# Splitting the per-pair selective-scan step of a Mamba layer into two halves, one pair apart

## What is computed

```python
def mamba(x):                       # W_in 1024x4096, DI = 2048
    xc, z = split(x @ W_in)
    u = silu(causal_depthwise_conv4(xc))
    dt_raw, B_raw = split(u @ W_x)  # 16 + 16
    dt = clip(softplus(dt_raw @ W_dt + b_dt), 1e-4, 1.0)
    ub = u * (B_raw @ W_Bp)
    h[t] = h[t-1] * (1 - dt[t]) + ub[t]
    y = (h + D_param * u) * silu(z)
    return y @ W_out
x = x + mamba(ln(x))
x = x + ffn(ln(x))                  # silu(x wg') * (x wu') @ wd', hidden 3072
x = x + attn(ln(x))                 # causal, one head of 1024, own residual
x = x + ffn(ln(x))
```

## Time and profile before

| | us |
|---|---|
| median of 2 runs | 3411.22 (3409.91 to 3412.52) |
| profiled execution | 3419.05 |
| its span on the slowest core (core 0) | 3417.5 |
| spans of the 8 cores | 3383.0 to 3417.5 |
| PE busy, of that span | 2018.6 (59%) |
| DVE busy | 956.0 (28%) |
| ACT busy | 776.5 (23%) |
| POOL busy | 323.6 (9%) |

### The profile page before, as it was taken

One profiled execution on the slowest core, in us unless ns is written; L12 is line 12 of the kernel. 1 busy time (PEld: TensorE's weight loads), 2 busy tenths in 40 slices (PEclk: granted clock), 3 DMA queues, 4 the chain that ended last, 5 costly groups with the idle time before them and its releaser, 6 DMA issues.

```text
span 3417.5 us, 29901 instructions; the slowest of 8 cores (3383.0 to 3417.5 us)
## 1 busy us (share of the span) xinstructions
PE 2018.6 (59%) x9275; PEld 984.6 (29%) x9432; DVE 956.0 (28%) x1617; ACT 776.5 (23%) x1196; POOL 323.6 (9%) x404
## 2 busy tenths in 40 slices
PE   1355555455554520764859577129677486859687
PEld 0233333333333210321324233014333142324232
DVE  3234444444444430102212120444322121211121
ACT  0244544445444423201101010100000110101010
POOL 0211222122222210021000000000000000000000
PEclk9576666676676655886989989559877698989889
DMA  7200000000000039243030302540211503030303
GB/s 243 73 13 25 1 25 7 19 25 1 25 7 19 22 123 289 77 136 120 16 108 1 98 26 71 172 154 1 86 51 48 181 23 101 13 111 1 110 13 96
DMA packets 69851, 233.31 MB, mean 68 GB/s; under 512 B 8450, under 2 KB 8578, under 8 KB 67652
## 3 DMA queue, kind: packets, MB, share of 16 engines
q10 hardware_dynamic: 35712, 112.21, 9.9%
q1 hardware_dynamic: 27460, 91.92, 8.9%
q0 software_dynamic: 6528, 27.27, 2.0%
HBM read 170.55 MB, written 60.82 MB: 68 GB/s over the span
## 4 chain that ended last, share of the span: by engine, by line
PE 38%; DMA 21%; DVE 13%; ACT 9%; issue 8%; DVEq 4%; POOLq 3%; POOL 2%; ACTq 2%; SPq 0%
PE ps_s L976 15%; DMA arena<-wd_c 6%; PE ps_s L942 5%; DVEq L143 4%; DMA arena<-xs 4%; PE ps_s L1046 3%; PE ps L1314 3%; PE ps L1046 3%; POOLq L143 2%; ACT L679 2%; POOL arena L560 2%; DVE arena L516 2%; PE ps_s L1261 2%; PE ps L759 2%; PE ps_s L1224 2%
## 5 line engine op out<-in xcount | busy, mean ns | idle before, releaser
L976 PE MATMUL ps_s<-arena 128*128 128x512 bf16 x2256 | 506.3, 385 | 10.8 <-DVE arena L328 8.6
L584 PE MATMUL ps_s<-arena 128*128 128x256 bf16 x1024 | 213.3, 396 | 336.8 <-ACT arena L508 334.4
L318 PE MATMUL ps<-arena 128*128 128x128 bf16 x512 | 63.5, 307 | 488.9 <-DVE arena L307 488.9
L976 PEld LDWEIGHTS ps_s<-arena 128*128 128x128 bf16 x2304 | 227.9, 99 | 287.8 <-issue 24.7
L1046 PE MATMUL ps_s<-arena 128*128 128x512 bf16 x752 | 210.4, 400 | 142.7 <-DMA arena<-wd_c 93.7
L266 ACT ACTIVATE arena<-arena 128x1024 bf16<-128x1024 f32 x64 | 67.6, 1057 | 917.2 <-DMA arena<-xs 826.4
L584 PEld LDWEIGHTS ps_s<-arena 128*128 128x128 bf16 x1024 | 136.5, 137 | 406.3 <-issue 353.7
L942 PE MATMUL ps_s<-arena 128*128 128x512 bf16 x752 | 170.3, 387 | 119.7 <-ACT arena L952 62.9
L499 PE MATMUL ps_s<-arena 128*128 128x256 bf16 x1024 | 172.9, 342 | 112.6 <-DVE arena L447 62.4
L991 DVE TENSOR_TENSOR arena<-arena,ps_s 128x512 bf16<-128x512 f32 x144 | 99.0, 688 | 422.2 <-ACT arena L985 422.2
L1046 PE MATMUL ps<-arena 128*128 128x512 bf16 x752 | 210.8, 402 | 0.9
(11 more groups left out here) (93 smaller groups left out, 2393.0 us busy)
## 6 DMA issues: line engine op xcount, KB each, us to landing
xs<-arena ACTq DMA_DIRECT2D x48, 512.0 KB, 2.9
arena<-xs ACTq DMA_DIRECT2D x48, 512.0 KB, 4.4
arena<-wd_c SPq DMA_DIRECT2D x84, 256.0 KB, 2.6
arena<-wd_c ACTq DMA_DIRECT2D x84, 256.0 KB, 2.6
arena<-wg_t SPq DMA_DIRECT2D x16, 768.0 KB, 6.2
arena<-wu_t SPq DMA_DIRECT2D x16, 768.0 KB, 6.6
arena<-x ACTq DMA_DIRECT2D x16, 512.0 KB, 4.6
arena<-w_in ACTq DMA_DIRECT2D x8, 1024.0 KB, 10.7
```

The source lines that it names most:

```text
L318: lambda e, s=xn_bf_tile, dj=dj, pbf=pbf: e.transpose(pbf[:, dj * P:(dj + 1) * P], s[:, dj * P:(dj + 1) * P], g_ident),
L584: lambda e, dj=dj, ci=ci, bkx=bkx, half=half, par=par: e.matmul(psb[bkx][:, half * TCM:(half + 1) * TCM], win_bf[:, dj * 4096 + ci * P: dj ...
L976: lambda e, hi=hi, dj=dj, bk=bk, par=par, wsrc=wsrc: e.matmul(psb[bk], wsrc[:, dj * H + hi * P: dj * H + (hi + 1) * P], fxnt[par][:, dj * ...
```

## The change

`phaseB_pair` becomes two functions. `phaseB1(k, pi)` holds the small matmuls, L674, the ACT chain and L691; `phaseB2(k, pi)` holds L697, the scan, L722, POOL's work and now, at its end, `wout_t0(k, pi)` of the same pair. The loop has nine steps: step `pi` emits B1 of pair `pi`, then B2 and phase A of pair `pi-1`. An unused view, `wd_pair`, goes. The computation and the waits are the same otherwise.

```diff
-        def phaseB_pair(k, pi):
+        def phaseB1(k, pi):
             ...
             mk_mm = s_pe.mark()
-            if pi >= 1:
-                wout_t0(k, pi - 1)
             em.op("vector",
             ...
-            mk_sp2 = mk_sp2_hist[(k, pi)] = s_se.mark()
+            mk_sp2_hist[(k, pi)] = s_se.mark()
             ...
             mk_ubm_hist[(k, pi)] = s_ve.mark()
+
+        def phaseB2(k, pi):
+            ci0 = 2 * pi
+            pp = pi % 2
+            prev_gp = mk_gp_hist.get((k, pi - 2)) or \
+                (mk_gp_hist.get((k - 1, 6 + pi)) if k > 0 else None)
             em.op("vector", lambda e, pp=pp: e.tensor_scalar(
                 a_f[pp][:], a_f[pp][:], 0.9999, None,
-                op0=ALU.min), wait=[mk_sp2], drain=False)
+                op0=ALU.min), wait=[mk_sp2_hist[(k, pi)]], drain=False)
             ...
             mk_gp_hist[(k, pi)] = s_gp.mark()
+            wout_t0(k, pi)
             ...
         for k in range(NKM):
-            for pi in range(8):
-                phaseB_pair(k, pi)
-                if k + 1 < NKM:
-                    phaseA_xc_pair(k + 1, pi)
-                    phaseA_z_pair(k + 1, pi)
+            for pi in range(9):
+                if pi < 8:
+                    phaseB1(k, pi)
+                if pi >= 1:
+                    phaseB2(k, pi - 1)
+                    if k + 1 < NKM:
+                        phaseA_xc_pair(k + 1, pi - 1)
+                        phaseA_z_pair(k + 1, pi - 1)
             if k + 1 == NKM - 1:
                 mk_xz_last = s_pe.mark()
-            wout_t0(k, 7)
             mamba_tail(k)
```

More of the change, by code:

```diff
@@ L815, in ffn @@
             wd_sb = [VA(F_WD + i * 2048, 2048, BF16) for i in range(2)]
-            wd_pair = VA(F_WD, 4096, BF16)
             fxA = [VA(F_XIN2 + i * 4096, 4096, F32) for i in range(NTF)]
```

## The result

The changed kernel takes 3451.84 us (median of 11 runs) for 3411.22 us of the kernel before; the ratio is 1.0117, with a 95% interval of 1.0084 to 1.0149: slower by a little over 1%, less than 2%. Some executions of every kernel here are several per cent slower at a lower granted clock, so the medians in this document are over all executions and the ratios over the others alone. The forecast was 3465 us in a range of 3412 to 3512. The two profiled executions took 3419.05 and 3443.83 us, 24.8 us apart; runs of one kernel differ by 13 us and more themselves (3399.29 to 3436.03 before, 3443.83 to 3456.39 after), so where the time went is read from stretches of the trace, and these repeat closely.

What follows compares the result with a forecast made beforehand. A ring through TensorE, closed by L643 waiting for y of the same pair, was to bound each step at 14.7 us; seven chunks (+40 us) and chunk 7 (+14) gave +54, 3465 us on the median, range 3412 to 3512.

Steps and rivals of the forecast that it cites:

- Ring one: Pair loop of ScalarE copy, DVE, GpSimd, SiLU and decay chain: 14.62 us before, some 11 us once split.
- the second ring: Loop through TensorE: L643 waits for same-pair y, behind DVE and the small matmuls; 16.4 us at the low clock.
- the signs that the prediction named: L643 waits for L735 in almost every pair, TensorE idle 5 to 6 us; first L508 15 us after L659.
- The step: One pair's round in chunks 0 to 6: 14.4 us with the clock rising, mean 14.7 us.
- one step in six: Share of pair steps expected to stay at the low clock throughout, raising the mean from 14.4 to 14.7 us.
- 5.78 + 0.5: Per step: 5.78 us of DVE and GpSimd work with TensorE idle, plus 0.5 us hold of L697 by L560.
- Fill, last step, end: Per chunk: 9.8 us before the first L643, 12.7 to the last burst, 8.6 from there to release.
- Chunk 7: Last chunk, with no next chunk to project: 66.6 us for 52.46, so +14 us.
- The tail: L747 to L769, the store and next layer norm after each chunk: unchanged, the edit costs nothing there.
- The low ring: Rival: clock stays low or the hold shifts each burst; steps 16.4 us, 3550 us in all; chance 0.18.
- The short ring: Rival: clock rises early, no hold on L697; steps 13.8 us, 3421 us in all; chance 0.16.
- The faster case: Rival: clock stays high across 5.8 us of idle; steps 12.4 us, chunks 101.3, 3332 us; chance 0.06.

Runs made afterwards that it cites:

- experiment 1: Changed kernel with the split kept, but output matmuls L643 again those of the pair before: 3218.10 us, ratio 0.9406.
- experiment 2: Changed kernel with the split kept, L643 of the same pair moved from ahead of L499 to behind L584: 3246.82 us, ratio 0.9484.
- experiment 3: Kernel before, not split, with L643 of the same pair placed ahead of L499: 3771.25 us in the profiled execution, no ratio.
- experiment 5: Changed kernel plus 26 matmuls into an unused bank ahead of each L643 in chunks 0 to 6: 3359.85 us, ratio 0.9850.

## Why the prediction was right

**The bound.** Ring one opened as forecast (57.6 to 0.4 us of wait), and the second ring closed in its place (52.8 us of L643 on y). Experiments 1 and 2 show that L643's place closes it, experiment 3 that it is the costly half. The "some 11 us" of the opened ring one came out as 11.1 to 11.4 in experiment 1. Of the signs that the prediction named, the wait of L643 was there in all eight pairs of chunk 1, and the first L508 of a chunk came 14.5 to 15.2 us after its L659; only the idle time ahead of L643 was above the 5 to 6 us given.

**The step.** 14.7 us forecast; measured 14.5 us in chunk 1 (87.3 us for six steps, from 342.9 to 430.2), which is the longest chunk, and 14.4 in the mean of all seven. Within it two terms were off and in part cancelled, which was luck. I had one step in six stay low altogether, worth 0.3 us; in none did it. In chunk 1 the clock rose in L499 or in the pause behind it every time (2.55 to 3.62 us for L499), and all of L584 took 1.91, as in the other six chunks. Against that the idle part was 6.4 to 6.7 us in these six steps, mean 6.5, and not 5.78 + 0.5: the hold on the clip was 0.55 to 0.83, and 0.05 us was missing in the releases.

In chunk 1 the hold is each time some 0.15 us less than what is left of the GpSimd instruction: at 367.14 us L560 had 0.70 us to go, and the clip lost 0.55. The prediction read the two L516 of the earlier trace rows as losing just what was left of L735; they lost 0.92 us, and 1.12 were left (357.44 + 1.15 less 357.47). The durations of the clip show the hold (minimum, median, maximum in ns; it was 426 to 428 in all 64 of before):

```profile
L701 DVE TENSOR_SCALAR arena<-arena x64: 417/980/1261, 195.4 to 1240.6; 128x512 f32<-128x512 f32 x64
```

**Fill, last step, end.** 9.8, 12.7 and 8.6 us forecast; 9.9, 12.8 and 7.5 measured in chunk 1, and 9.8, 13.1 and 7.7 in the mean of seven. The end was shorter since L584 was at the high clock there too. Per chunk 119.3 us forecast, 116.7 measured: +3.2 for +5.7.

**Chunk 7.** 66.6 us forecast, 67.6 measured: +15.2 for +14.

**The tail** is the one step whose reasoning failed: "so this edit costs nothing" stood for L747 to L769, and the tail got shorter. Seven such stretches took 8.6 to 10.3 us before, 65.2 in sum, and 8.6 to 9.0 after, 60.6 in sum. Before, the output matmuls of the second half (L759) began at the low clock in three of the seven chunks and took 8.50 to 8.75 us there, for 7.07 in the other four. Chunk 0 of before:

```profile
304.96 1.02 PE L643 MATMUL ps<-arena 128*128 128x512 bf16 x4 [0.71 <-POOL arena L735]
...
307.52 8.56 PE L759 MATMUL ps<-arena 128*128 128x512 bf16 x31 [1.54 <-DVE arena L747]
```

The same chunk after, where L764 is L759 and takes 6.85 us in all seven chunks:

```profile
304.71 1.91 PE L584 MATMUL ps_s<-arena 128*128 128x256 bf16 x16 [0.82 <-ACT arena L508]
...
308.38 6.85 PE L764 MATMUL ps<-arena 128*128 128x512 bf16 x31 [1.76 <-DVE arena L752]
```

So before, L643 still ran at the high clock (1.02 us for four), and it was gone after 1.54 us of idle time; in the other four chunks the same pause did not bring it down, nor did the 1.76 us after the change. Why is not shown. These 4.6 us and 2.4 us from elsewhere between the chunks, which I did not trace, are the 7 us that came back. With the shorter chunks they make the difference between +54 forecast and +30.5 in the Mamba layer. The direction and the mechanism were right; of the 54 us forecast 40.6 are there between the medians and 24.8 between the profiled executions.

**The rivals.** The low ring (16.4 us a step) did not come, as no step stayed low. The short ring (13.8) did not either, as the hold was there in all six steps of every chunk. The faster case needed a clock that outlasts the idle time; it did not, but experiment 5, which fills that time, came to its numbers: 12.45 us a step for 12.4, chunks of 102.8 for 101.3.

**A hold in the last step.** No row of before showed an instruction with two SBUF inputs held by GpSimd. The changed kernel has one in the last step of a chunk, where the scans of pair 7 meet the two GpSimd sums of pair 6 (here chunk 6):

```profile
1153.99 1.26 POOL L555 TENSOR_TENSOR arena<-arena 128x512 f32<-128x512 f32 x1 [6.95 <-ACT arena L546]
1154.15 3.25 DVE L707 TENSOR_TENSOR_SCAN arena<-arena 128x256 f32<-128x256 f32 x2
1155.41 1.44 POOL L560 TENSOR_TENSOR arena<-arena 128x512 f32<-128x512 f32 x1 [0.16 <-issue]
```

The two scans take 3.25 us here and 1.39 alone, so 1.9 us are lost once a chunk. I had left 0.3 us for holds in this step. It still took 12.8 us in chunk 1 and 13.1 in the mean, for the 12.7 of the forecast, so its other links had been priced more than 1 us too long: this term came out by luck. The Trainium skill (SBUF — State Buffer, "Who interferes with whom") says that a DVE instruction with two SBUF inputs contends with a GpSimd instruction that reads SBUF. By that rule I had put the loss at 1.3 us, on top of the sum; the trace agrees that the scans are held, and the loss is 1.9.

## What to carry to other kernels

When a step is split so that its slow half runs one round ahead, look at what each in-order queue now has in front of its next independent work: here four matmuls that ask for this round's result turned a 6% gain into a 1% loss, and leaving them one round behind brought it back. Write the ring down engine by engine, with each link's duration at the clock it will get, before and after; a wait that vanishes from the list of waits tells nothing until the next ring's length is known. The ring through TensorE paid for its idle time twice here: 6.4 us a step as such, and another 2.1 in the low clock of what followed (experiment 5).

## What had not been expected

- Work that leaves the result alone made a kernel faster, which I expected only once I had the trace of the changed kernel: 26 added matmuls a step took the chunks from 116.7 to 102.8 us, and the whole from 1.0117 to 0.9850 of the kernel before.
- The clock rose at about the same place in every step of the changed kernel, within L499 or in the 0.8 us pause behind it, and no step stayed low, where I had one in six: L584 took 1.91 us in each of the eight pairs of all seven chunks, where before it had begun low behind every long idle stretch.
- A hold by GpSimd does not vanish when the held instruction is moved away; the scan, 1.39 us for two, took 1.65 to 1.93 in its place in nearly every step.
